# RNN input by eight-step block products from step 40 instead of 48, LSTM input by pairs from step 16 instead of 20

## The reference

```python
def step(prev_h, xw):                      # RNN; xw = x_t @ Wx + b, h0 = cond_1024
    next_h = jnp.tanh(prev_h @ Wh + xw)
x = x + rnn(x)

def step(carry, xw_t):                     # LSTM; xw_t = x_t @ Wx + b, h0 = c0 = 0
    a = xw_t + prev_h @ Wh                 # 32 x 2048
    i, f, o = sigmoid of the first three quarters of a; g = tanh of the last
    next_c = f * prev_c + i * g
    next_h = o * jnp.tanh(next_c)
x = x + lstm(x)
```

## Time and profile before

| what | value |
|---|---|
| median of 3 runs | 838.79 us (836.5, 838.79, 839.27) |
| the profiled execution's own time | 839.34 us |
| its span, first to last instruction | 837.5 us |
| granted TensorE clock | 1.00 throughout |
| busy: PE, PEld, DVE, ACT, POOL | 98%, 73%, 77%, 73%, 40% |

### The profile page before, as it was taken

One profiled execution on the slowest core, in us unless ns is written; L12 is line 12 of the kernel. 1 busy time (PEld: TensorE's weight loads), 2 busy tenths in 40 slices (PEclk: granted clock), 3 DMA queues, 4 the chain that ended last, 5 costly groups with the idle time before them and its releaser, 6 DMA issues.

```text
span 837.5 us, 52092 instructions
## 1 busy us (share of the span) xinstructions
PE 822.3 (98%) x22620; PEld 611.0 (73%) x22620; DVE 648.0 (77%) x1794; ACT 612.3 (73%) x1637; POOL 331.5 (40%) x693
## 2 busy tenths in 40 slices
PE   7899999999999999999999999999999999999997
PEld 4555555677777887777777777777777777777796
DVE  3689778877898777878888787888878787767764
ACT  4896576766778778787877878787787878777752
POOL 1222466734544334343433434343343434333310
PEclk9999999999999999999999999999999999999999
DMA  8711101110011111111111111111111101011001
GB/s 294 266 52 27 29 15 28 29 29 23 11 29 30 29 31 27 42 42 35 46 30 35 26 42 42 33 47 34 29 30 42 42 21 37 17 33 26 13 8 28
DMA packets 54580, 36.21 MB, mean 43 GB/s; under 512 B 9788, under 2 KB 52944, under 8 KB 53072
## 3 DMA queue, kind: packets, MB, share of 16 engines
q1 hardware_dynamic: 54096, 32.78, 14.3%
q10 hardware_dynamic: 256, 0.11, 0.0%
...
## 4 chain that ended last, share of the span: by engine, by line
PE 86%; DVE 5%; DMA 4%; ACT 3%; issue 2%; SPq 0%; ACTq 0%; DVEq 0%
PE ps_l L1602 33%; PE ps_l L1677 27%; PE ps_r L1803 9%; PE ps_l L1655 5%; PE ps_pk L1786 3%; PE ps_end L1786 2%; PE ps_r L1823 2%; PE ps_l L1615 2%; DMA whl_raw<-in_L_cond_Wh 2%; DMA wxl_raw<-in_L_cond_Wx 2%; DMA wxr_raw<-in_L_cond_Wx 1%; DVE wxl_lo L1354 1%; ACT wxl_hi L879 0%; ACT wxl_lo L857 0%; DVE fc L1379 0%
## 5 line engine op out<-in xcount | busy, mean ns | idle before, releaser
L594 POOL TENSOR_TENSOR xb<-xb,h_l 128x128 f32<-128x128 f32 x127 | 58.2, 458 | 379.6 <-DVE h_lo L1414 371.3
L1677 PE MATMUL ps_l<-whl_raw,wxl_raw 128*32 128x256 f16 x3816 | 131.8, 273 | 0.0
L1602 PE MATMUL ps_l<-whl_hi,hT_hi 128*32 128x512 f16 x1888 | 122.6, 379 | 0.0
L1602 PE MATMUL ps_l<-whl_lo,hT_hi 128*32 128x512 f16 x1888 | 122.5, 379 | 0.0
L1602 PE MATMUL ps_l<-whl_hi,hT_lo 128*32 128x512 f16 x1888 | 122.5, 379 | 0.0
L1677 PE MATMUL ps_l<-wxl_hi,wxl_raw 128*32 128x256 f16 x2544 | 115.9, 273 | 0.5 <-ACT ps_l L842 0.5
L1677 PEld LDWEIGHTS ps_l<-whl_raw,wxl_raw 128*32 128x32 f16 x3816 | 102.2, 97 | 2.2
L1602 PEld LDWEIGHTS ps_l<-whl_lo,hT_hi 128*32 128x32 f16 x1888 | 50.8, 97 | 51.2
L1602 PEld LDWEIGHTS ps_l<-whl_hi,hT_lo 128*32 128x32 f16 x1888 | 50.8, 97 | 51.2
L998 ACT ACTIVATE gates<-ps_l,g_products 128x256 f32<-128x256 f32 x115 | 54.1, 470 | 46.5 <-PE ps_l L1602 46.5
L1677 PEld LDWEIGHTS ps_l<-wxl_hi,wxl_raw 128*32 128x32 f16 x2544 | 68.4, 97 | 18.3 <-ACT ps_l L842 1.0
...
## 6 DMA issues: line engine op xcount, KB each, us to landing
xb<-in_x SPq DMA_DIRECT2D x128, 64.0 KB, 2.1
...
whl_raw<-wxl_lo SPq DMA_DIRECT2D x160, 32.0 KB, 2.3
...
```

What stands on the lines that cost most here:

```text
L594: nc.gpsimd.tensor_tensor(xb[g % NX][:, t, :], xb[g % NX][:, t, :], h_l[s % 2][:, :], ALU.add).then_inc(out_done, 1)
L1602: last = nc.tensor.matmul(ps_l[s % 4][quarter(j), :], (hT_hi, hT_lo)[h_part][:, k, :], gate_slice(whl[w_part][k], j), start=False, stop=(h ...
L1677: last = nc.tensor.matmul(at[quarter(j), :], stationary, weights[:, j, :, :], start=False, stop=(y_part == 1 and k == 1), skip_group_check ...
```

## The change

It moves both block schemes to an earlier step, and with them the ticks of all the preparation. `S2` goes from 20 to 16, so that two more pairs replace four single-step products; `XQ` from 6 to 5, so that one more set of seven block products replaces eight single-step RNN products. Which operation stands where:

- T blocks: GpSimd makes four pieces a tick in ticks 13 to 20 instead of three in 14 to 24; the halves are in ticks 14 to 17 and 19 to 22.
- RNN weight blocks: two GpSimd operations per tick in ticks 22 to 25; one conversion per tick in ticks 27, 28, 30 and 31.
- Peaks: the third batch (tick 26) covers groups 8 and 9 alone, and a first batch by DMA for groups 10 and 11 is added at tick 25. The peaks of groups 2 and 3 go from ScalarE to VectorE (ticks 7, 8), that of 5 stays in tick 10, those of 6 and 7 go to tick 11.
- Weights: the last low half of the LSTM's input weight goes from late in tick 10 to tick 11; the RNN's recurrent weight goes from ticks 10 (ScalarE) and 11 (VectorE) to ticks 11 and 12 (ScalarE, in two parts) and 12 (VectorE). A high half and a bound change ticks (6 and 7).
- `y_lo` of group 1 stands behind the RNN's turn; the turn of x group 4 goes from tick 12 to 13.
- `product_l(5)` is cut in three: 16 matmuls in tick 11 ahead of the RNN's products, 28 behind them, and 4 in tick 12 inside the recurrent product of step 5, which is itself cut.
- On TensorE the RNN's input product of the next step comes before its recurrent product from tick 13 on instead of 26. `LOW_FIRST` goes from 27 to 23.

```diff
-S2 = 20
+S2 = 16
-XQ = 6
+XQ = 5
-        BATCHES = [(G1, 3), (4, 4), (8, 4)] + [(g, 2) for g in range(GX, NG, 2)]
+        BATCHES = [(G1, 3), (4, 4), (8, 2)] + [(g, 2) for g in range(GX, NG, 2)]
-        TURN_X_AT.update({4 * g - 4: g for g in range(3, GX)})
+        TURN_X_AT.update({4 * g - 4: g for g in range(3, GX) if g != 4})
+        TURN_X_AT[13] = 4
-        W_LOW_AT = {6: [(OF_H, 0), (OF_H, 1)], 7: [(OF_H, 2), (OF_H, 3)], 9: [(OF_X, 1)], 10: [(OF_X, 2)]}
-        W_LOW_LATE_AT = {8: [(OF_X, 0)], 10: [(OF_X, 3)]}
-        R_LOW_AT = {5: OF_X, 11: OF_H}
-        PEAK_ON_ACT_AT = {3: [1], 7: [2], 8: [3], 9: [4], 10: [5, 6, 7]}
-        R_HIGH_AT = {5: OF_X, 10: OF_H}
+        W_LOW_AT = {6: [(OF_H, 0), (OF_H, 1)], 7: [(OF_H, 2), (OF_H, 3)], 9: [(OF_X, 1)], 10: [(OF_X, 2)], 11: [(OF_X, 3)]}
+        W_LOW_LATE_AT = {8: [(OF_X, 0)]}
+        R_LOW_AT = {5: OF_X, 12: OF_H}
+        PEAK_ON_ACT_AT = {3: [1], 9: [4], 10: [5], 11: [6, 7]}
+        PEAK_LATE_AT = {7: 2, 8: 3}
+        R_HIGH_AT = {5: OF_X}
+        R_HIGH_H_AT = (11, 12)
-        XW_AT = {27 + i: i for i in range(8)}
-        XW_HALVES_AT = {36: (0, 1), 38: (2, 3)}
-        BIAS_X_AT, XIN_ZERO_AT = 35, {41: 0, 43: 1}
-        LOW_FIRST = 27
+        XW_AT = {22 + i: (2 * i, 2 * i + 1) for i in range(4)}
+        XW_HALVES_AT = {27: (0,), 28: (1,), 30: (2,), 31: (3,)}
+        BIAS_X_AT, XIN_ZERO_AT = 27, {33: 0, 35: 1}
+        LOW_FIRST = 23
-        T_MADE_AT = {14 + i: range(3 * i, min(32, 3 * i + 3)) for i in range(11)}
-        T_HIGH_AT = {k: [(T_ORDER[i // 2], i % 2)] for i, k in enumerate((17, 18, 19, 21, 22, 23, 24, 25))}
+        T_MADE_AT = {13 + i: range(4 * i, 4 * i + 4) for i in range(8)}
+        T_HIGH_AT = {k: [(T_ORDER[i // 2], i % 2)] for i, k in enumerate((14, 15, 16, 17, 19, 20, 21, 22))}
-        CONST_AT = 23
+        CONST_AT = 19
...
+            def first_of_halves(part):
+                if part == 0:
+                    pe.wait_ge(l_seeded, S1 - N0 + 1)
+                    pe.wait_ge(y_high, 1)
+                    pe.wait_ge(w_high[OF_X], J)
+                    for k in range(J):
+                        chunk_product(S1, 0, 0, k)
+                if part == 1:
+                    pe.wait_ge(w_split[OF_X], J - 1)
+                    for k in range(J - 1):
+                        chunk_product(S1, 0, 1, k)
+                    pe.wait_ge(y_split, 1)
+                    for k in range(J):
+                        chunk_product(S1, 1, 0, k)
+                if part == 2:
+                    pe.wait_ge(w_split[OF_X], J)
+                    chunk_product(S1, 0, 1, J - 1).then_inc(xl_mm, 1)
...
-                if 1 <= k - LAG < S3:
+                if k - LAG == S1:
+                    recurrent_l(S1, ((0, 0), (0, 1)))
+                elif 1 <= k - LAG < S3:
                     recurrent_l(k - LAG)
...
+                if k - LAG == S1:
+                    first_of_halves(2)
+                    recurrent_l(S1, ((1, 0),))
+                if k - LAG + 1 == S1:
+                    first_of_halves(0)
...
-                if k >= IN_PAIRS:
+                if k >= R0:
                     next_product_r(k + 1)
                 if LAG < k < R0:
                     recurrent_r(k)
                 if R0 <= k < T:
                     recurrent_r16(k)
-                if LAG <= k < IN_PAIRS:
+                if LAG <= k < R0:
                     next_product_r(k + 1)
                 if k - LAG + 1 == S1:
-                    product_l(S1)
+                    first_of_halves(1)
```

More of the change, by code:

```diff
@@ L1638, in product_f32, with chunk_product @@
                     last.then_inc(xl_mm, 1)
+            def chunk_product(s, y_part, w_part, k):
+                g, t = group(s)
+                for j in range(J):
+                    last = nc.tensor.matmul(ps_l[s % 4][quarter(j), :], y16[y_part][g % 2][:, k, t * B:(t + 1) * B],
+                                            gate_slice(wxl[w_part][k], j), start=False, stop=False, skip_group_check=True)
+                return last
+            def first_of_halves(part):
[15 more added lines that the diff above has]
+                    chunk_product(S1, 0, 1, J - 1).then_inc(xl_mm, 1)
             def product_l(s):
```

48 lines of the change are left out of this document (26 added, 22 removed).

## The result

| | before | after |
|---|---|---|
| median of six executions each | 838.38 us (836.5 to 839.27) | 842.84 us (840.39 to 844.12) |
| ratio | | 1.0051, interval 1.0035 to 1.0067 |
| the profiled execution's own time, its span | 839.34, 837.5 | 840.78, 839.0 |

The kernel became slower by 4.5 us; 835.2 was forecast, and 842.84 lies above the range (832.9 to 838.6). The profiled execution of after is one of its short ones: TensorE begins tick 9 at 51.26 us there and at 52.93 in the one of before. From the start of tick 9 to the start of tick 47 the two profiles differ by 258.65 - 255.32 = 3.3 us, and the text goes by that.

The account below looks back on a forecast made before the run. TensorE, busy 98% of the span, was taken as the bound, with 4.5 us of waits. 839.34 - 1.86 - 1.0 + 0 - 0.7 = 835.8, or 835.2 on the median's scale; range 832.9 to 838.6.

Parts of the forecast that it names:

- Reading of before: TensorE's ticks 11 to 45: 6.49 us single-step, 6.19 pairs, 6.85 with a block product; waits in four places only.
- Part 1: TensorE's matmuls: two more pairs save 1.2 us, one more set of block products 0.66; together -1.86.
- Part 2: Ticks 11 to 13: of 1.6 us lost waiting, -1.0 net, between +0.3 and -1.6.
- The 0.4 to 0.5 that I set for tick 14: Loss at tick 14 because tick 13 takes over a turn of x beside the scales and a peak.
- the sign of being right: Ticks 11 to 14 together 27 to 28 us instead of 28.65, tick 11 near 6.7, tick 12 near 7.2.
- Part 3: T blocks in ticks 13 to 22: denser GpSimd pieces and moved halves cost 0, between -0.2 and +2 us.
- ScalarE's wait for the constants in tick 20: GpSimd falls behind, so ScalarE waits over 1 us in tick 20, with no gap on TensorE.
- Part 4: Ticks 24 to 39, conversions one per tick and moved exchanges: -0.7 us, between -1.6 and +1.2.
- new waits in ticks 27 to 31: 0.7 to 0.8 us, since exchanges, a conversion and scales add 2.1 on VectorE, more than the 0.7 of room.
- The slower rival: VectorE becomes the bound in ticks 13 to 31, with denser GpSimd work; 840.5 us, chance 0.10.
- The rule: VectorE with two SBUF inputs and GpSimd block each other on a shared port; sum 1 to 3 us higher.

Follow-up runs that it names:

- e6: Kernel before with the changes of ticks 6 to 13 alone; ratio 0.9996 to before.
- e18: Kernel before with only the RNN block conversions spread one per tick, in ticks 35, 36, 38, 39; ratio 0.9997 to before.
- e5: Kernel after with the RNN's block products starting at step 48 again, their pieces and conversions as before; ratio 1.0033 to before.
- e11: Kernel after with GpSimd's T pieces over 8 columns instead of 256; ratio 1.0008 to before.
- e7: Kernel before with the T blocks alone moved, four pieces a tick in ticks 13 to 20 and halves in 14 to 17, 19 to 22; 843.45 us, ratio 1.0046.
- e14: Kernel after with two of each tick's four T pieces moved to the end of GpSimd's queue; ratio 1.004 to before.

## Why the prediction was wrong

- **Reading of before**: the tick lengths 6.49, 6.19 and 6.85 came back after the change. One reading was off by a tick: "ticks 14 to 23 already hold 30 pieces and six low halves" counts the program's ticks against TensorE's. In TensorE's ticks 14 to 23, the 64.90 us, nine groups of three pieces (27) and five low halves run; the sixth begins at 155.00, in tick 24.
- **Part 1** (-1.86, matmuls): held. Ticks 31 to 45 and 46 show the moved products at their price, and tick 46 is 0.63 shorter.
- **Part 2** (-1.0): sign right, 0.6 of it came. Tick 11 came to 6.71, as worked out. Tick 12 took 7.96 instead of 7.2: the matmuls that I left for it waited 0.64 for wxl_lo where I had 0.3 at most, and the two matmuls of the exchange (0.38) stand in it too. In all 0.6 gained. The 0.4 to 0.5 that I set for tick 14 was zero when this part stood alone (e6). In after tick 14 took 7.28, and ticks 11 to 14 together 28.9 where 27 to 28 was the sign of being right: the room that this part took was missing once the T blocks and the new order on TensorE came as well (6.92 with short pieces, 6.71 with the old order).
- **Part 3** (0, between -0.2 and +2): **the step that failed.** It cost 3.8 in ticks 14 to 18, and 3.6 in ticks 9 to 46 when made alone (258.94 - 255.32). Tick 22 lost 1.05 more, where the prediction carried over 0.45. ScalarE's wait for the constants in tick 20 came as worked out (1.31, no gap on TensorE). I counted GpSimd's own queue and found it fit, and took ten ticks without loss as proof that a denser packing has none. They only showed slack: hT_hi was ready 0.6 to 1.2 before the next tick, and that is all the room there was. A sign of what would use it stood in the earlier trace rows: fc at 412 ns beside three pieces a tick instead of 300; fc, ig and c together came to 1564 ns with four, instead of 926. I also never laid the T halves' new ticks against what else stands there: in the program's tick 14 x's low half on VectorE and x's high half on ScalarE, in 16 a turn of x and y's low half (TensorE's ticks 15 and 17, the two longest). In before no T half stood in the program's tick 14, 16 or 20.
- **Part 4** (-0.7): came out at about +0.8, inside its own bounds: -1.3 in ticks 37 to 39 as forecast, -0.1 in ticks 26 to 30, and 2.15 more in ticks 23 to 25, which the sum did not have. The two conversions in a tick were worth 0.8 of the 1.3 (e18). Of the 0.7 to 0.8 of new waits in ticks 27 to 31 only 0.1 came (tick 27 took 6.62, as in before). But for GpSimd's two block pieces a tick the sum had nothing: ticks 22 to 25 lost 3.2, and 2.15 of that is the block pieces' (after against e5).
- **The slower rival** named the right mechanism and place, "VectorE becomes the bound in ticks 13 to 31", and its time (840.5) was too low by 2.3. Its terms were 3.2 for ticks 13 to 20 (3.8 in 14 to 18), 0.8 for ticks 22 to 25 (3.2) and 1.3 for tick 27 (nothing). I had put it at 0.10 because "ten ticks with three pieces each show no loss at all"; a queue with 0.6 to 1.2 us of room shows no loss until it is full, and then every tick adds.
- **The rule** (the Trainium skill, "SBUF — State Buffer", Who interferes with whom: VectorE with two SBUF inputs and GpSimd reading SBUF exclude each other, whoever comes second waits for the whole instruction) was priced at 1 to 3 us, and I left it out of the sum. The trace agrees with it: fc and ig beside a block piece of 1.2 to 1.3 take 1.25 and 1.35 instead of 0.28, y's low half 1.49 instead of 0.70, and a turn of x, with one input, keeps its 1.11 beside the T pieces. By e11 the pieces carry 2.9 in ticks 14 to 18 alone, so the 1 to 3 us belonged in the sum.

What stays open: the 0.95 of ticks 14 and 15, and tick 22's 7.24, where TensorE waits 0.86 for the RNN's low half of h. Behind the cell on VectorE, that half comes late by a T half (1.41), a peak (0.63) and y's low half (0.94) in the same tick. In e7 the tick behind the first pair's has no T half and takes 6.20, against 6.73 in before, and in e14 y's low half took 0.70 and tick 22 6.97; no run took the T half out of tick 22 in after. Open, too, are the 1.2 us between the 4.5 of the medians and the 3.3 of the stretches: behind tick 46 the two profiles take 529.29 and 529.06, start-up scatters (tick 9 began between 51.26 and 53.86), and the kernel before, timed again beside the experiments, had medians of 838.65 to 839.55 instead of 838.38.
